# Where the next table's products stand in the block loop of a gather layer

## The chip, the cores and the metric

The kernel runs on one core of a Trainium2 chip. Its metric is the device time of one execution in microseconds, the median of several runs. PE is TensorE (PEld its weight loads), DVE is VectorE, ACT is ScalarE, POOL is GpSimd and SP is SyncE. The profiled execution has times on the chip for every instruction.

## The reference

A graph with 6,250 nodes of 256 features and 100,000 edges, sorted by destination, each edge with one of eight relation types. The part that matters here is the two-layer graph network:

```
xn = layernorm(x)
for l in 0, 1:
    W[r] = sum_b coeffs[l, r, b] * bases[l, b]        # eight 256 x 256 matrices
    h[r] = x @ W[r]                                   # 6250 x 256 each
    msg  = h[edge_type, src] / max(deg[dst], 1)
    x    = segment_sum(msg, dst) + x @ self_loops[l]  # relu behind l = 0
```

Beside it, linear attention needs, over all nodes, the sum of outer products of keys and values of xn; the rest (second layer, attention output, a routed two-matrix expert network) comes behind and is the same before and after.

## The kernel before

`h` of a layer is kept in DRAM as a table of 6272 x 8 rows of 256 floats. `startup` normalizes x, turns it and writes the first table. `gnn_first` is the first gather layer and at the same time writes the second table, that is, it multiplies each finished block of 128 nodes with the next layer's eight matrices. `gnn_second` then gathers from that table, and `experts` ends the kernel.

`gnn_first` loops over NB = 49 blocks of 128 destination nodes. The engines run their own instruction lists, in program order, and meet at semaphores. `reach(eng, sem)` waits until a semaphore has risen by one more than this engine last waited for.

- **POOL** (`Aggregate.gather`, L487) has only gathers: one indirect DMA for each 128 edges fetches their rows of the table to a ring of 16 groups of four such tiles. When the ring is full it waits, once for two groups, until PE has begun the sums of the groups that are to be overwritten.
- **SP** (`count`) passes on which groups have landed, and issues some fills with zeros.
- **DVE** makes the one-hot matrices of a block's edges (`onehots`, L510 and L514, double buffered), then `finish` (L633 to L639: degree, reciprocal, scale and add own, relu, giving `xn`) and `front` (L643, L644: bias of keys and values). `low_part` (L623) makes the low part of the split of the block's turned values, and `keys` (L628) the key features.
- **PE**, for block b: `own` (L690, self loop), `sum` (L530: four matmuls for each group, one-hot times ring, between two matmuls by zero, L523 and L537), `project` (L696: keys and values), `outer` of the block before (L703), `multiply` of the block before (L715) and `turn` (L722, two transposes of `xn`). `multiply` has four chunks of 512 columns with six matmuls each (high by high, high by low, low by high, for two halves). Two PSUM banks take the chunks in turn, so chunk 2 waits until ACT has copied chunk 0.
- **ACT**: `high_part` (L754 x1T from PSUM, L756 the rounded high part), `own_part` (L763), `keep` (L759, DMA), `store` (L769, four chunk copies, then L780, a DMA of 1024 KB to the table) and the two activations of the keys (L794, L795).

The turn of block b goes out at the end of PE's step b, and its product in step b + 1, behind the sums of block b + 1. In the last step both remaining products follow the turn. The releaser names that the trace gives for semaphores can be those of an earlier stage whose semaphore numbers are used again: `pre_bs<-in_L_gnn_bases` is a tensor of `startup`.

Of the kernel before, what the change touches and what calls it, by code (L numbers as in the profile page):

```python
# [540 lines left out]
def gnn_first(nc, g, a):  # L541
# [3 lines left out]
    with ExitStack() as ctx:  # L545
# [67 lines left out]
        @block.vector  # L613
        def _(eng):
            V = nc.vector

            def seq(ins):
                ins.then_inc(dve_own, 1)
                reach(eng, dve_own)

            def low_part(k):
                reach(eng, high_ok)
                V.tensor_tensor(low[:, k, :, :], x1T[:, k, :, :], high[:, k, :, :],  # L623
                                ALU.subtract).then_inc(low_ok, 1)

            def keys(k):
                reach(eng, er_ok)
                V.scalar_tensor_tensor(out=kf[:, k, :], in0=ke[:, k, :], scalar=1.0, in1=kr[:, k, :],  # L628
                                       op0=ALU.min, op1=ALU.add).then_inc(kf_ok, 1)

            def finish(b, k):
                reach(eng, agg.agg_ok)
                seq(V.tensor_scalar(dm[:, :], agg.pagg[:, k, D:D + 1], 1.0, None, ALU.max))  # L633
                seq(V.reciprocal(g.dinv[:, ds(b, 1)], dm[:, :]))
                reach(eng, own_ok)
                seq(V.scalar_tensor_tensor(out=xn[:, :], in0=agg.pagg[:, k, 0:D], scalar=g.dinv[:, ds(b, 1)],
                                           in1=own[:, :], op0=ALU.mult, op1=ALU.add))
                eng.sem_inc(agg.agg_free, 1)
                V.tensor_scalar(xn[:, :], xn[:, :], 0.0, None, ALU.max).then_inc(xn_ok, 1)  # L639

            def front(k):
                reach(eng, p_ok)
                V.tensor_tensor(kt[:, k, :], pk[:, 0:D], bkv[:, 0:D], ALU.add).then_inc(kt_ok, 1)  # L643
                V.tensor_tensor(vb[:, k, :, 0:P], pk[:, D:2 * D].rearrange("p (h n) -> p h n", h=H2),  # L644
                                bkv[:, D:2 * D].rearrange("p (h n) -> p h n", h=H2), ALU.add).then_inc(p_free, 1)

            def step(b, k, prev):
                agg.onehots(eng, b, seq)
                if prev:
                    low_part(1 - k)  # L650
                    keys(1 - k)
                finish(b, k)
                front(k)
                if b == NB - 1:
                    low_part(k)

            eng.sem_inc(p_free, 1)
            agg.begin(eng)
            V.memset(zrow[:, :], 0.0).then_inc(zrow_ok, 1)
            eng.wait_ge(zrow_ok, 1)  # L660
            V.memset(zrow[:, D:D + 1].bitcast(I32), SKIP).then_inc(zrow_ok, 1)
            seq(V.memset(vb[:, :, :, P:P + 2], 1.0))
            seq(V.memset(mask[:, :], 0.0))
            for h in range(P // HD):
                ins = V.memset(mask[h * HD:(h + 1) * HD, h * HD:(h + 1) * HD], 1.0)
            seq(ins)
            for h in range(H2):
                eng.wait_ge(split_ok, h + 1)
                ins = V.tensor_tensor(wlow[:, h, :], rows[:, h, :], whigh[:, h, :], ALU.subtract)
            ins.then_inc(split_ok, 1)  # L670
            eng.wait_ge(kv_in, 80)
            for b in range(NB):
                step(b, b % 2, b > 0)
            keys((NB - 1) % 2)
            agg.end(eng)

            eng.wait_ge(kv_done, 1)
            for h in range(H2):
                V.tensor_tensor(g.kvn[:, h, 0:P], pkv[:, h * D:h * D + P], mask[:, :], ALU.mult)
                ins = V.tensor_copy(ksum[:, h:h + 1], pkv[:, h * D + P:h * D + P + 1])  # L680
            seq(ins)
            for h in range(H2):
                ins = V.tensor_scalar(g.kvn[:, h, P:], mask[:, 0:P:HD], ksum[:, h:h + 1], None, ALU.mult)
            seq(ins)

        @block.tensor
        def _(eng):
            def own(b):
                for h in range(H2):
                    mm = nc.tensor.matmul(po[:, 0:D], g.xT[:, h, b * P:(b + 1) * P], ws[:, h, :], start=(h == 0), stop=(h == H2 - 1))  # L690
                mm.then_inc(own_ps, 1)

            def project(b):
                reach(eng, p_free)
                for h in range(H2):
                    mm = nc.tensor.matmul(pk[:, :], g.xT[:, h, b * P:(b + 1) * P], wkv[:, h, :], start=(h == 0), stop=(h == H2 - 1))  # L696
                mm.then_inc(p_ok, 1)

            def outer(k, last=False):
                reach(eng, kf_ok)  # L700
                n = LAST if last else P
                for h in range(H2):
                    mm = nc.tensor.matmul(pkv[:, h * D:h * D + P + 2], kf[0:n, k, h * P:(h + 1) * P], vb[0:n, k, h, :],  # L703
                                          start=False, stop=(last and h == H2 - 1), skip_group_check=True)
                if last:
                    mm.then_inc(kv_done, 1)

            def multiply(k):
                reach(eng, low_ok)
                x, w = (high[:, k, :, :], low[:, k, :, :]), (whigh, wlow)  # L710
                for n in range(2 * W):
                    reach(eng, chunk_free)
                    for h in range(H2):
                        for i, j in ((0, 0), (0, 1), (1, 0)):
                            mm = nc.tensor.matmul(pm[:, n % W, 0:CW], x[i][:, h, :], w[j][:, h, n * CW:(n + 1) * CW],  # L715
                                                  start=(h == i + j == 0), stop=(h == H2 - 1 and i == 1))
                    mm.then_inc(chunk_ok, 1)

            def turn():
                reach(eng, xn_ok)  # L720
                for h in range(H2):
                    mm = nc.tensor.transpose(pT[:, h * P:(h + 1) * P], xn[:, h * P:(h + 1) * P], g.ident[:, :])  # L722
                mm.then_inc(xT_ps, 1)

            def step(b, k, prev):
                own(b)
                agg.sum(eng, b, k)
                project(b)
                if prev:
                    outer(1 - k)  # L730
                if b < NB - 1:
                    if prev:
                        multiply(1 - k)
                    turn()
                else:
                    turn()
                    multiply(1 - k)

            reach(eng, agg.ring_ok)
            eng.wait_ge(kv_in, 80)  # L740
            eng.wait_ge(split_ok, H2 + 1)
            nc.tensor.matmul(pkv[:, 0:2], g.zero[:, :], g.zero[:, 0:2], start=True, stop=False, skip_group_check=True)
            for b in range(NB):
                step(b, b % 2, b > 0)
            multiply((NB - 1) % 2)
            outer((NB - 1) % 2, last=True)
            eng.sem_inc(agg.groups_in, -NG)

        @block.scalar
        def _(eng):  # L750
            def high_part(k):
                reach(eng, kept[k], 16)
                reach(eng, xT_ps)
                nc.scalar.copy(x1T[:, k, :, :], pT[:, 0:D].rearrange("p (h n) -> p h n", h=H2)).then_inc(x1T_ok, 1)  # L754
                reach(eng, x1T_ok)
                nc.scalar.copy(high[:, k, :, :], x1T[:, k, :, :]).then_inc(high_ok, 1)  # L756
# [22 lines left out]
                lo = W * CW if b == NB - 1 else 0  # L779
                eng.dma_start(table_rows(g, 1, b)[:, lo:], rows[:, k, lo:]).then_inc(stored[k], 16)  # L780

            def step(b, k, prev):
                if prev:
                    high_part(1 - k)
                own_part()
                if prev:
                    keep(b - 1, 1 - k)
                if b == NB - 1:
                    high_part(k)
                    keep(b, k)  # L790
                if prev:
                    store(b - 1, 1 - k)
                reach(eng, kt_ok)
                nc.scalar.activation(ke[:, k, :], kt[:, k, :], ACT.Exp)  # L794
                nc.scalar.activation(kr[:, k, :], kt[:, k, :], ACT.Relu).then_inc(er_ok, 1)  # L795

            eng.sem_inc(chunk_free, W)
            for k in range(2):
# [2 lines left out]
            eng.wait_ge(wr_in, WEIGHTS_IN)  # L801
            for h in range(H2):
                nc.scalar.copy(whigh[:, h, :], rows[:, h, :]).then_inc(split_ok, 1)
            for b in range(NB):
                step(b, b % 2, b > 0)
            store(NB - 1, (NB - 1) % 2)
            for k in range(2):
                reach(eng, stored[k], 32 if k == (NB - 1) % 2 else 16)
                reach(eng, kept[k], 16)
# [521 lines left out]
```

## Time and profile before

| what | value |
|---|---|
| three runs, median (lowest to highest) | 3634.85 us (3616.99 to 3636.49) |
| profiled execution, its own time | 3627.62 us |
| its span in the trace | 3625.9 us |
| mean granted clock of TensorE | 0.801 |
| PE busy | 2399.8 us, 66% |
| POOL busy | 1649.7 us, 45% |
| DVE, ACT busy | 915.7 us, 652.3 us |
| gathers of both layers (L487) | 1564 |

Busy time of an engine is the union of its instructions' times. A PE matmul's end is modelled, so its start is the firmer number. DMA-issuing instructions count as the queue's own (ACTq) and not as busy time, but for POOL's gathers. Times in the rows count from the span's start.

### The profile page before, as it was taken

The numbers are of one execution on the slowest core, as the hardware profiler recorded it, in microseconds if no ns is written. First come the engines' busy times: TensorE is split into PE (matmuls) and PEld (weight loads), VectorE is DVE, ScalarE is ACT, GpSimd is POOL, SyncE is SP. The second block draws the span as 40 slices with busy tenths as digits, with TensorE's granted clock in tenths as the row PEclk, the third lists the DMA queues.
The fourth block names the chain that finished last, engine by engine and source line by source line (L and its number), as shares of the span: only waits on it lengthen the run. The fifth ranks groups of instructions, "written<-read, shape, count | busy, mean of one in ns | idle before, by whom it ended". The sixth has DMA issues, their size and how long they took to land. (4 is left out here: it accounts for less than half of the span.)

```text
span 3625.9 us, 37652 instructions
## 1 busy us (share of the span) xinstructions
PE 2399.8 (66%) x9592; PEld 1739.3 (48%) x9592; DVE 915.7 (25%) x2885; ACT 652.3 (18%) x1423; POOL 1649.7 (45%) x1712
## 2 busy tenths in 40 slices
PE   6999346666666666666578356676666667657287
PEld 3777234444444444444456244454444545445065
DVE  2210112222222222222123023233332323324233
ACT  4555101110111011111111101111212112110033
POOL 0000654445444444445451646556565555652535
PEclk9999668878887888778789678777777777878577
DMA  8655533333333333333332323333333333321341
GB/s 220 231 218 195 156 95 112 106 107 103 112 102 104 103 110 109 106 103 113 100 121 75 121 77 92 89 88 91 87 90 88 89 92 89 90 84 46 128 128 53
DMA packets 155518, 401.32 MB, mean 111 GB/s; under 512 B 35102, under 2 KB 86657, under 8 KB 140348
## 3 DMA queue, kind: packets, MB, share of 16 engines
q0 software_dynamic: 81648, 219.65, 20.8%
q10 hardware_dynamic: 36156, 126.22, 9.0%
q1 hardware_dynamic: 37585, 53.92, 5.5%
q8 instruction: 58, 0.95, 0.1%
q14 instruction: 71, 0.58, 0.1%
HBM read 262.69 MB, written 141.04 MB: 111 GB/s over the span
## 5 line engine op out<-in xcount | busy, mean ns | idle before, releaser
L487 POOL DMA_INDIRECT gnn_ring<-table,g_idx x1564 | 1513.1, 967 | 1627.0 <-PE gnn_pagg L530 857.3
L530 PE MATMUL gnn_pagg<-gnn_ring,gnn_oh 128*128 x3904 | 1124.5, 432 | 427.7 <-issue 378.6
L530 PEld LDWEIGHTS gnn_pagg<-gnn_ring,gnn_oh 128*128 128x128 f32 x3904 | 775.7, 212 | 775.3 <-issue 662.9
L514 DVE TENSOR_TENSOR gnn_oh<-gnn_col,g_dst 128x256 f32<-128x256 f32 x976 | 408.3, 426 | 1803.6 <-DVEq L49 1609.9
L715 PE MATMUL gnn_pm<-gnn_whigh,gnn_high 128*128 128x512 f32 x392 | 202.4, 516 | 480.1 <-ACT gnn_rows L769 473.1
L769 ACT COPY gnn_rows<-gnn_pm 128x512 f32<-128x512 f32 x196 | 110.9, 587 | 1320.9 <-DMA pre_bs<-in_L_gnn_bases 1082.7
L715 PEld LDWEIGHTS gnn_pm<-gnn_whigh,gnn_high 128*128 128x128 f32 x392 | 94.4, 241 | 520.0 <-ACT gnn_rows L769 493.4
L1026 ACT ACTIVATE gnn_qe<-gnn_pq,gnn_bq 128x128 f32<-128x128 f32 x98 | 36.0, 368 | 1061.1 <-remote 1045.6
L715 PE MATMUL gnn_pm<-gnn_wlow,gnn_high 128*128 128x512 f32 x392 | 188.0, 480 | 0.0
L715 PE MATMUL gnn_pm<-gnn_whigh,gnn_low 128*128 128x512 f32 x392 | 186.7, 476 | 0.0
L366 PE MATMUL pre_psum<-pre_whigh,pre_high 128*128 128x512 f32 x392 | 157.5, 402 | 10.6 <-DVE pre_low L294 8.1
L366 PE MATMUL pre_psum<-pre_whigh,pre_low 128*128 128x512 f32 x392 | 153.7, 392 | 0.0
L366 PE MATMUL pre_psum<-pre_wlow,pre_high 128*128 128x512 f32 x392 | 153.3, 391 | 0.0
L417 ACT COPY pre_rows<-pre_psum 128x512 f32<-128x512 f32 x196 | 114.6, 589 | 118.1 <-PE pre_psum L366 108.4
L1131 POOL DMA_INDIRECT out<-g_xT x80 | 80.0, 1000 | 99.9 <-DVE g_xT L1208 78.8
L715 PEld LDWEIGHTS gnn_pm<-gnn_whigh,gnn_low 128*128 128x128 f32 x392 | 94.9, 242 | 25.0
L715 PEld LDWEIGHTS gnn_pm<-gnn_wlow,gnn_high 128*128 128x128 f32 x392 | 96.4, 246 | 18.7
L696 PE MATMUL gnn_pk<-gnn_wkv,g_xT 128*128 128x512 f32 x196 | 98.0, 623 | 0.0
L1125 POOL DMA_INDIRECT bucket<-rt_x,exp_posi x49 | 51.2, 1045 | 89.4 <-DVE exp_posi L1229 74.7
L366 PEld LDWEIGHTS pre_psum<-pre_whigh,pre_high 128*128 128x128 f32 x392 | 74.1, 189 | 25.1 <-DVE pre_low L294 8.5
L366 PEld LDWEIGHTS pre_psum<-pre_whigh,pre_low 128*128 128x128 f32 x392 | 73.9, 188 | 15.9
L366 PEld LDWEIGHTS pre_psum<-pre_wlow,pre_high 128*128 128x128 f32 x392 | 74.2, 189 | 14.2
(172 smaller groups left out, 2210.0 us busy)
## 6 DMA issues: line engine op xcount, KB each, us to landing
table<-pre_rows ACTq DMA_DIRECT2D x49, 1024.0 KB
table<-gnn_rows ACTq DMA_DIRECT2D x48, 1024.0 KB
gnn_ring<-table,g_idx POOLq DMA_INDIRECT x1564
pre_bs<-in_L_gnn_bases SPq DMA_DIRECT2D x64, 240.0 KB
bucket<-gnn_zrow SPq DMA_DIRECT2D x16, 650.0 KB
g_xT<-bucket SPq DMA_DIRECT2D x20, 520.0 KB, 6.3
x1T<-gnn_x1T ACTq DMA_DIRECT2D x49, 128.0 KB
gnn_x1T<-x1T ACTq DMA_DIRECT2D x49, 128.0 KB, 2.1
```

What stands on the lines that cost most here:

```text
L366: mm = nc.tensor.matmul(psum[:, n, 0:hi - lo], x[i][:, h, :], w[j][:, h, lo:hi], start=(h == i + j == 0), stop=(h == H2 - 1 and i == 1))
L417: nc.scalar.copy(rows[:, b % 2, lo:hi], psum[:, n, 0:hi - lo]).then_inc(chunk_free, 1)
L487: eng.indirect_dma_start(self.ring[:, q % RG, t, 0:D], None, self.g.table[self.l][:, :], bass.IndirectOffsetOnAxis(ap=self.g.idx[:, at:at ...
L514: self.nc.vector.tensor_tensor(self.oh[:, h, :, :], self.col[:, :].unsqueeze(1).to_broadcast([P, n, P]), self.g.dst[:, ds(q * TPG + h * n, ...
L530: mm = nc.tensor.matmul(pagg[:, k, 0:self.width], self.oh[:, h, i, :], self.ring[:, ds(q & (RG - 1), 1), t, 0:self.width].rearrange("p o n ...
L696: mm = nc.tensor.matmul(pk[:, :], g.xT[:, h, b * P:(b + 1) * P], wkv[:, h, :], start=(h == 0), stop=(h == H2 - 1))
L715: mm = nc.tensor.matmul(pm[:, n % W, 0:CW], x[i][:, h, :], w[j][:, h, n * CW:(n + 1) * CW], start=(h == i + j == 0), stop=(h == H2 - 1 and ...
L769: ins = nc.scalar.copy(rows[:, k, n * CW:(n + 1) * CW], pm[:, n % W, 0:CW])
L1026: nc.scalar.activation(qe[:, k, h, :], pq[:, h * P:(h + 1) * P], ACT.Exp, bias=bq[:, h:h + 1])
L1125: eng.indirect_dma_start(g.bucket[:, :], bass.IndirectOffsetOnAxis(ap=posi[:, b:b + 1], axis=0), r.x2[:, b, :], None).then_inc(scattered, 16)
L1131: eng.indirect_dma_start(out[:, :], bass.IndirectOffsetOnAxis(ap=xb[:, t % XS, D:D + 1].bitcast(I32), axis=0), xb[:, t % XS, 0:D], None, b ...
```

## The change

PE's step b becomes: `own(b)`, `outer` of block b - 2, `multiply` of block b - 1, `sum(b)`, `project(b)`, `turn`. So a block's product comes right behind its own turn (with only the next block's own matmuls and an older outer product between) and ahead of the next block's sums. Behind the loop follow the outer product of block NB - 2, the product and the outer product of the last block. DVE's step ends with this block's `low_part` and `keys`; before, they stood one block later, behind the one-hots. ACT's step begins with this block's `high_part`; then `own_part` of the next block, the two activations, `keep` and `store` of this block. The first `own_part` stands ahead of the loop. No buffer, no operation and no amount of data changes.

```diff
--- before.py
+++ after.py
@@ -644,15 +644,12 @@
                 V.tensor_tensor(vb[:, k, :, 0:P], pk[:, D:2 * D].rearrange("p (h n) -> p h n", h=H2),
                                 bkv[:, D:2 * D].rearrange("p (h n) -> p h n", h=H2), ALU.add).then_inc(p_free, 1)
 
-            def step(b, k, prev):
+            def step(b, k):
                 agg.onehots(eng, b, seq)
-                if prev:
-                    low_part(1 - k)
-                    keys(1 - k)
                 finish(b, k)
                 front(k)
-                if b == NB - 1:
-                    low_part(k)
+                low_part(k)
+                keys(k)
 
             eng.sem_inc(p_free, 1)
             agg.begin(eng)
@@ -670,8 +667,7 @@
             ins.then_inc(split_ok, 1)
             eng.wait_ge(kv_in, 80)
             for b in range(NB):
-                step(b, b % 2, b > 0)
-            keys((NB - 1) % 2)
+                step(b, b % 2)
             agg.end(eng)
 
             eng.wait_ge(kv_done, 1)
@@ -722,26 +718,23 @@
                     mm = nc.tensor.transpose(pT[:, h * P:(h + 1) * P], xn[:, h * P:(h + 1) * P], g.ident[:, :])
                 mm.then_inc(xT_ps, 1)
 
-            def step(b, k, prev):
+            def step(b, k):
                 own(b)
+                if b >= 2:
+                    outer(k)
+                if b >= 1:
+                    multiply(1 - k)
                 agg.sum(eng, b, k)
                 project(b)
-                if prev:
-                    outer(1 - k)
-                if b < NB - 1:
-                    if prev:
-                        multiply(1 - k)
-                    turn()
-                else:
-                    turn()
-                    multiply(1 - k)
+                turn()
 
             reach(eng, agg.ring_ok)
             eng.wait_ge(kv_in, 80)
             eng.wait_ge(split_ok, H2 + 1)
             nc.tensor.matmul(pkv[:, 0:2], g.zero[:, :], g.zero[:, 0:2], start=True, stop=False, skip_group_check=True)
             for b in range(NB):
-                step(b, b % 2, b > 0)
+                step(b, b % 2)
+            outer(NB % 2)
             multiply((NB - 1) % 2)
             outer((NB - 1) % 2, last=True)
             eng.sem_inc(agg.groups_in, -NG)
@@ -779,20 +772,15 @@
                 lo = W * CW if b == NB - 1 else 0
                 eng.dma_start(table_rows(g, 1, b)[:, lo:], rows[:, k, lo:]).then_inc(stored[k], 16)
 
-            def step(b, k, prev):
-                if prev:
-                    high_part(1 - k)
-                own_part()
-                if prev:
-                    keep(b - 1, 1 - k)
-                if b == NB - 1:
-                    high_part(k)
-                    keep(b, k)
-                if prev:
-                    store(b - 1, 1 - k)
+            def step(b, k):
+                high_part(k)
+                if b < NB - 1:
+                    own_part()
                 reach(eng, kt_ok)
                 nc.scalar.activation(ke[:, k, :], kt[:, k, :], ACT.Exp)
                 nc.scalar.activation(kr[:, k, :], kt[:, k, :], ACT.Relu).then_inc(er_ok, 1)
+                keep(b, k)
+                store(b, k)
 
             eng.sem_inc(chunk_free, W)
             for k in range(2):
@@ -801,9 +789,9 @@
             eng.wait_ge(wr_in, WEIGHTS_IN)
             for h in range(H2):
                 nc.scalar.copy(whigh[:, h, :], rows[:, h, :]).then_inc(split_ok, 1)
+            own_part()
             for b in range(NB):
-                step(b, b % 2, b > 0)
-            store(NB - 1, (NB - 1) % 2)
+                step(b, b % 2)
             for k in range(2):
                 reach(eng, stored[k], 32 if k == (NB - 1) % 2 else 16)
                 reach(eng, kept[k], 16)
```

## Rows read from the trace of the kernel before

**Rows 1.** Table of stages, chosen stretches: length, busy us of PE, PEld, DVE, ACT, POOL, granted clock, DMA share, GB/s.

```profile
480.00:1920.00 1440.00, 929.52 (x3494) 671.99 (x3495) 310.36 (x835) 169.26 (x389) 682.29 (x704) 0.81 0.33 107
...
1920.00:2010.00 90.00, 83.84 (x358) 62.67 (x356) 28.96 (x86) 20.95 (x46) 6.01 (x6) 0.99 0.23 86
...
911.00:915.00 4.00, 3.85 (x19) 2.88 (x17) 1.18 (x3) 1.66 (x5) 0.22 (x1) 1.00 0.73 295
```

**Rows 2.** Chain of waits, 480 to 1920 us: us in total, times, longest.

```profile
ACT gnn_rows L769 <- DMA pre_bs<-in_L_gnn_bases: 1082.7, 48, 45.5
...
POOL gnn_ring L487 <- PE gnn_pagg L530: 544.7, 43, 16.5
```

**Rows 3.** Timeline of POOL: start, us, what, count, idle before and its releaser.

```profile
882.38 1.13 POOL L487 DMA_INDIRECT gnn_ring<-table,g_idx  x1 [13.83 <-PE gnn_pagg L530]
...
901.54 0.95 POOL L487 DMA_INDIRECT gnn_ring<-table,g_idx  x1 [0.31 <-issue]
...
914.78 1.13 POOL L487 DMA_INDIRECT gnn_ring<-table,g_idx  x1 [12.30 <-PE gnn_pagg L530]
```

**Rows 4.** Timeline of PE, 889 to 911 us.

```profile
889.15 0.17 PE L537 MATMUL gnn_pagg<-g_zero 128*128 128x2 bf16 x1
...
891.34 0.47 PE L715 MATMUL gnn_pm<-gnn_whigh,gnn_high 128*128 128x512 f32 x1
...
893.95 0.39 PE L715 MATMUL gnn_pm<-gnn_whigh,gnn_low 128*128 128x512 f32 x1
...
905.79 0.79 PE L715 MATMUL gnn_pm<-gnn_whigh,gnn_high 128*128 128x512 f32 x1 [11.45 <-ACT gnn_rows L769]
...
906.81 0.63 PE L715 MATMUL gnn_pm<-gnn_whigh,gnn_low 128*128 128x512 f32 x1
...
907.23 0.63 PE L715 MATMUL gnn_pm<-gnn_whigh,gnn_high 128*128 128x512 f32 x1
...
910.06 0.38 PE L722 MATMUL gnn_pT<-g_ident,gnn_xn 128*128 128x128 f32 x2
...
911.14 0.17 PE L523 MATMUL gnn_pagg<-g_zero 128*128 128x2 bf16 x1
```

**Rows 5.** Timeline of ACT, 905 to 911 us.

```profile
905.15 1.07 ACT L769 COPY gnn_rows<-gnn_pm 128x512 f32<-128x512 f32 x2 [24.95 <-DMA pre_bs<-in_L_gnn_bases]
...
910.95 0.33 ACTq L780 DMA_DIRECT2D table<-gnn_rows  x1
```

**Rows 6.** Timeline of DVE, 892 to 896 us.

```profile
892.38 0.16 DVE L633 TENSOR_SCALAR gnn_dm<-gnn_pagg 128x1 f32<-128x1 f32 x1 [3.87 <-remote]
...
893.41 0.38 DVE L639 TENSOR_SCALAR gnn_xn<-gnn_xn 128x256 f32<-128x256 f32 x1
...
895.80 0.76 DVE L514 TENSOR_TENSOR gnn_oh<-gnn_col,g_dst 128x256 f32<-128x256 f32 x2 [0.40 <-issue]
```

**Rows 7.** Timeline of PE and ACT, 926 to 938 us.

```profile
926.41 0.39 PE L715 MATMUL gnn_pm<-gnn_whigh,gnn_low 128*128 128x512 f32 x1
...
932.31 0.59 ACT L769 COPY gnn_rows<-gnn_pm 128x512 f32<-128x512 f32 x1 [19.30 <-DMA pre_bs<-in_L_gnn_bases]
...
937.86 1.08 ACT L769 COPY gnn_rows<-gnn_pm 128x512 f32<-128x512 f32 x2 [4.96 <-DMA pre_bs<-in_L_gnn_bases]
```

**Rows 8.** Timeline of the loop's last block, 1992 to 2006 us.

```profile
1992.10 0.17 PE L537 MATMUL gnn_pagg<-g_zero 128*128 128x2 bf16 x1
...
1994.38 0.38 PE L722 MATMUL gnn_pT<-g_ident,gnn_xn 128*128 128x128 f32 x2
...
1994.85 0.37 ACT L754 COPY gnn_x1T<-gnn_pT 128x256 f32<-128x256 f32 x1 [9.14 <-PE gnn_pT L722]
...
1995.25 0.41 ACT L756 CAST gnn_high<-gnn_x1T 128x256 fp32r<-128x256 f32 x1
...
1995.69 0.42 DVE L623 TENSOR_TENSOR gnn_low<-gnn_x1T,gnn_high 128x256 fp32r<-128x256 f32 x1 [0.81 <-ACT gnn_high L756]
...
2005.57 0.61 PE L703 MATMUL gnn_pkv<-gnn_vb,gnn_kf 106*128 106x130 f32 x4
```

## The prediction

> **What bounds the kernel now.** I read the table of stages first [rows 1]. In the first layer's loop, 480 to 1920 us, PE is busy 929.5 of 1440 us and POOL 682.3, so no engine is full. In the 90 us behind it, where POOL issues six gathers, PE is busy for 83.8. The profiled execution took 3627.62 us with a span of 3625.9; this loop is 40% of it, and the change touches nothing else.
>
> The chain of waits says who stands still for whom [rows 2]: POOL waits 43 times for the sums, 544.7 us in all, and ACT's copies of the product chunks wait 1082.7 us for something named after a DMA of the stage before. So POOL works in bursts, one about every 1440/43 = 33.5 us. The burst of [rows 3] runs from the gather at 882.38 to the one started at 901.54: 16 gathers in 19.16 us.
>
> What ACT's copy waits for has to be found by exclusion. Its two conditions are the store of two blocks ago and the chunk itself. The store is not late: one issued at 910.95 falls into a stretch of 4 us that moves 295 GB/s, 1.18 MB, enough for its 1024 KB [rows 1, 5]. And in one block the first copy ran at 932.31 and the next at 937.86 although only the chunk's semaphore lies between them and chunk 1's last matmul was issued at 926.41 [rows 7]. So PE's completions are reported late. In the block of [rows 4, 5], chunks 0 and 1 are issued from 891.34 to 893.95, and both are copied from 905.15: 11 us later, and 3.61 us after the start of the burst's last gather [rows 3]. Where no burst runs, a turn issued at 1994.38 is copied at 1994.85 [rows 8]. Why completions are held the trace doesn't tell; that they are let go at the burst's end is what I build on. I call that moment E.
>
> One block is then: the sums start at T; the first gather at T+3.6 (911.14, 914.78 [rows 3, 4]); the last one 19.2 later; E 3.6 after that; then what PE still owes before the next sums. That last stretch is 905.15 to 911.14 here, 5.99 us, and 33.5-26.4 = 7.1 on the average. **It is exposed, and it is what the change edits.** It holds 0.64 us of copy and handoff (to 905.79), the 12 matmuls of chunks 2 and 3 (4.27 us, to 910.06), then the turn and own (1.08 us, to 911.14) [rows 4].
>
> **The change part by part: PE.** The same matmuls run per block in another order: sums, project, turn, next block's own, an outer product one block later than before, all four chunks, sums. Chunk 0 of a block now hangs on that block's own turn, x1T copy, split and low part. When is the turn done? The sums' last matmul is issued at 889.15 and reported at 892.38; the relu of xn starts at 893.41 and takes 0.38 [rows 4, 6]. So the turn goes out 11.5 us into the burst, and PE stands still before it for some 3 us; that costs nothing, as PE then has 10 us of burst to wait out. Chunk 0 of before was issued in the same place, second behind the sums, 10.3 us into the burst, and was held to E. I take it that the turn is held to E as well, and own behind it.
>
> Then, from E: copy to split 0.40 us (1994.85, 1995.25), split to low part 0.44 (to 1995.69), low part 0.42 and a handoff of about 0.07 [rows 8]: 1.33 us to the first chunk matmul. Behind it 24 matmuls instead of 12. PE has stood still for 11 us before them as it had before 905.79, and there its matmuls start 0.42 us apart (906.81, 907.23), 512 columns at the 1.2 GHz level, before they reach 0.237 (11 steps from 891.34 to 893.95) [rows 4]. That slow start is paid once in either order. So the first 12 matmuls cost 4.27 as now, the other 12 cost 12 x 0.237 = 2.84. Gone are 0.64 and 1.08. **Sum: 1.33+2.84-0.64-1.08 = +2.4 us a block.**
>
> The bounds of it: were the 12 extra matmuls all at the low level, 12 x 0.42 = 5.0 us, it would be +4.6; were all 24 at the full one, 1.33+5.7 = 7.0 against 7.1, nothing. The row at 905.79 is the nearest, as it shows a restart after the same pause.
>
> *How many blocks.* 43 bursts, but in five of them the first copy came well before the burst's usual end; the one at 932.31 is such a block [rows 7]. There the turn may be answered in time, and I take nothing for them: 38 x 2.4 = **+91 us**.
>
> *The ends of the loop.* Now two products follow the last sums, from 1992.10 to 2005.57. After the change one does: the turn at about 1993.9, the chunks 0.47+1.33 later, 24 x 0.23 = 5.5 us, so 2001.2: **-4.4 us** [rows 8]. The three blocks before, without bursts, wait 1.8 us from turn to chunks and have own and an outer product (about 1.5) to fill it: +0.3 each, +0.8. At the start the first product falls into the long first filling of the ring, in which the second block's sums waited anyway: +1.5, from 0 to 5.
>
> **DVE.** low_part and keys are moved, not added, from behind the next block's one-hots to ahead of them. Behind low_part's new wait stand keys and those one-hots, and for them the next sums. Low ends at E+1.3; keys waits for ke and kr, which ACT does behind x1T, split and own, each up to the split's 0.40, so it ends near E+2.5; from relu to the first one-hot, with two other operations between, it is 2.4 us now (893.41, 895.80) [rows 6], so the one-hot is there by E+5.4. The sums start at E+9.5. The chunks hide it; without them it would be those 5.4 us.
>
> **ACT.** Its x1T copy waits at the head of the block, with split, own, ke and kr behind, then the chunk copies: they are free at about E+2, and chunk 0 is through at E+4. The table store leaves about 1 us after the next sums have started, not 0.19 before (910.95, 911.14) [rows 4, 5]. It moves for 4 us and would overlap the burst's first 1.4 us; that bounds a late burst at +1.4, and I take 0, since the burst's pace, 19.16/15 = 1.28 us a gather, is POOL's issue and not the data's. POOL's and SP's queues keep their order.
>
> 3627.6+91-4.4+0.8+1.5 = 3716.5. The median of the runs shown lies 7 us above the profiled time, within their spread of 19.5. I predict **3718 us**.
>
> **The rivals.** *A, the turn is held to E*: above, 3718; from +1.6 to +3.6 a block, 3685 to 3765.
>
> *B, the turn comes through, own doesn't.* Completions also come singly inside a burst (932.31, two gathers before its end [rows 7]). Chunks 0 and 1 would then be done at E, but ACT owes own, ke and kr first, 1.3 us or so: E to sums 1.3+0.64+4.27 = 6.2 against 5.99 here, +0.2 a block, about 3640.
>
> *C, faster: nothing of the turn is held.* If turn and own are answered in 0.5 us as in [rows 8], chunks 0 and 1 stand ready at E, ACT owes nothing, and the sums start 0.64+4.27 later: 1.08 less a block, 43 x 1.08 = 46, less 2 at the ends: 3580. It decides once the turn and own are reported 5 us ahead of E. For it: the sums inside a burst get their answers at once, or the one-hots would not keep up. Against it: 905.15, which is what 38 of 43 blocks do. The Trainium skill (SBUF — State Buffer, Who interferes with whom) states that a DMA never contends with a compute engine, since engine and DMA ports are apart. By that rule gathers could not hold PE's work back and C would come true; the rows at 893.95 and 905.15 don't agree with so wide a reading, as something about the burst does reach PE's reports.
>
> *D, worse: the low clock lasts through the whole product.* 43 x 4.6 = 198: 3824. Against it: after 905.79 twelve matmuls took 4.27, not 5.0.
>
> **How the numbers follow.** About 0.5%, 18 us, is what a measurement can tell from no change. A 0.68, B 0.12, C 0.12, D 0.08. A rests on a row that repeats in most blocks; that the turn inherits chunk 0's fate is my inference, and B and C share what it leaves. Slower is A and D, 0.76; same is B, 0.12; faster is C, 0.12. The range leaves out C and D, 0.20, and ends a little beyond B and A: 3625 to 3775.
>
> **What would show each step.** If A is right, no chunk matmul runs inside a burst, the x1T copy comes 3.6 us after the last gather's start, and 24 chunk matmuls follow in about 7 us; POOL's waits grow from 544.7/43 = 12.7 to 15 us, the distance of bursts from 33.5 to 35.9. The stretch from the last sums to the layer's end shrinks by 4 us. I am wrong at the main step if x1T copies lie well inside the bursts (B if own's doesn't, C if both do), at the size if chunk matmuls stay 0.42 apart (D), and at the cover if the sums' first matmul waits for a one-hot.

## The result, and the profile after

The changed kernel takes **3594.66 us** (median of 8 runs, 3585.02 to 3609.15), the kernel before 3631.37 beside it (8 runs): 0.9916 of before, 95% interval 0.9891 to 0.9941. It is faster by 0.8%, where the prediction said slower. The profiled execution took 3602.8 us with a span of 3601.1, 24.8 us less span than the kernel before has in its trace.

The table of stages has the loop of the first layer (columns as in [rows 1]):

```profile
480.00:1920.00 1440.00, 993.40 (x3607) 700.30 (x3608) 324.51 (x855) 181.93 (x407) 687.51 (x710) 0.86 0.34 109
```

In the same 1440 us PE issues more matmuls than in [rows 1], 3607, at a granted clock of 0.86 instead of 0.81, and POOL more gathers, 710: more blocks go through in that time. The chain of waits of the same stretch:

```profile
POOL gnn_ring L487 <- PE gnn_pagg L530: 541.6, 47, 16.9
ACT gnn_x1T L747 <- DMA pre_rows<-wrel: 348.5, 20, 33.3
ACT gnn_rows L762 <- DMA pre_bs<-in_L_gnn_bases: 257.1, 42, 14.5
ACT gnn_x1T L747 <- PE gnn_pT L718: 231.9, 16, 16.2
ACT gnn_own L756 <- remote: 102.8, 40, 4.8
```

POOL still waits for PE's sums once a block, but ACT's wait of 1082.7 us for the chunks [rows 2] is down to 257.1. ACT now stands at the x1T copy instead, the head of its block, where the engine has nothing else to do. "remote" and the DMAs of long past stages are the profile's guesses at what released these waits; what they have in common is that a completion of PE is seen late.

The timeline of one block, POOL, PE, ACT and DVE together (start, length, engine, idle time before):

```profile
879.59 1.13 POOL L487 DMA_INDIRECT gnn_ring<-table,g_idx  x1 [11.49 <-PE gnn_pagg L530]
886.36 0.17 PE L537 MATMUL gnn_pagg<-g_zero 128*128 128x2 bf16 x1
889.59 0.16 DVE L633 TENSOR_SCALAR gnn_dm<-gnn_pagg 128x1 f32<-128x1 f32 x1 [4.54 <-remote]
891.03 0.44 PE L718 MATMUL gnn_pT<-g_ident,gnn_xn 128*128 128x128 f32 x2 [2.68 <-DVE gnn_xn L639]
893.19 0.37 ACT L747 COPY gnn_x1T<-gnn_pT 128x256 f32<-128x256 f32 x1 [16.47 <-DMA pre_rows<-wrel]
894.51 0.79 PE L711 MATMUL gnn_pm<-gnn_whigh,gnn_high 128*128 128x512 f32 x1 [1.49 <-issue]
896.69 0.37 ACT L756 COPY gnn_own<-gnn_po 128x256 f32<-128x256 f32 x1 [2.69 <-remote]
898.64 0.94 POOL L487 DMA_INDIRECT gnn_ring<-table,g_idx  x1 [0.30 <-issue]
899.31 0.39 PE L711 MATMUL gnn_pm<-gnn_whigh,gnn_low 128*128 128x512 f32 x1
902.46 1.07 ACT L762 COPY gnn_rows<-gnn_pm 128x512 f32<-128x512 f32 x2 [4.77 <-DMA pre_bs<-in_L_gnn_bases]
903.10 0.80 PE L711 MATMUL gnn_pm<-gnn_whigh,gnn_high 128*128 128x512 f32 x1 [3.40 <-ACT gnn_rows L762]
...
907.31 0.18 PE L523 MATMUL gnn_pagg<-g_zero 128*128 128x2 bf16 x1
...
908.20 0.33 ACTq L773 DMA_DIRECT2D table<-gnn_rows  x1
910.96 1.13 POOL L487 DMA_INDIRECT gnn_ring<-table,g_idx  x1 [11.38 <-PE gnn_pagg L530]
```

The burst runs from 879.59 to 898.64. The turn goes out at 891.03, and **its answer is there at 893.19, inside the burst**, 9 us before E. Own's comes at 896.69. So chunks 0 and 1 are through PE by 899.7, and they, and they alone, are held to E (902.46, 3.8 us behind the start of the last gather). From there to the sums it is 4.85 us, against 5.99 in [rows 4, 5].

Over the 44 intervals of the loop's 45 bursts, the time from a burst's first gather to the next sums adds up to 1278.8 us before and 1238.7 after: 40.1 less, 0.91 a burst. The turn's copy starts 2.2 us after the turn (median of the 42 bursts of 16 gathers), own's 5.6 us after the turn (mean).

### The profile page after: what moved, and what is told of

Its sections match the earlier page's. It is cut to its first block and busy times, and to the rows that moved or that the text cites. A ratio compares the mean times of both kernels' runs of the same rounds, so it can differ in the third digit from the quotient of the medians.

```text
span 3601.1 us, 37652 instructions
## 1 busy us (share of the span) xinstructions
PE 2442.1 (68%) x9592; PEld 1750.2 (49%) x9592; DVE 924.5 (26%) x2885; ACT 657.0 (18%) x1423; POOL 1648.2 (46%) x1712
## 5 line engine op out<-in xcount | busy, mean ns | idle before, releaser
L711 PE MATMUL gnn_pm<-gnn_whigh,gnn_low 128*128 128x512 f32 x392 | 194.7, 497 | 0.0
L762 ACT COPY gnn_rows<-gnn_pm 128x512 f32<-128x512 f32 x196 | 110.7, 587 | 449.4 <-DMA pre_bs<-in_L_gnn_bases 257.1
L747 ACT COPY gnn_x1T<-gnn_pT 128x256 f32<-128x256 f32 x49 | 18.2, 372 | 802.7 <-DMA pre_rows<-wrel 391.4
L718 PE MATMUL gnn_pT<-g_ident,gnn_xn 128*128 128x128 f32 x98 | 21.7, 304 | 98.2 <-DVE gnn_xn L639 56.3
```

The lines of the kernel that those rows point to most:

```text
L762: ins = nc.scalar.copy(rows[:, k, n * CW:(n + 1) * CW], pm[:, n % W, 0:CW])
```

## The experiments

The runs are of two kinds, and this has to be known to read them. Each set of kernels ran together on one chip, with the kernel before among them. In some sets the kernel before took 3613 to 3672 us, with bursts as above; in others some 2612 us, and POOL hardly paused. The kind was the same for every kernel and execution of a set. The chip alone doesn't settle it: chip 4 showed only bursts, 0 and 5 only the other kind, 12 each once. Every ratio below is to the kernel before in the same set. The changed kernel and the kernel before it were traced only with bursts, and the changed kernel was never timed without them.

**1. Where the gain is: only turn and own moved.** The product is the one of the block before, so two products follow the last sums again; the rest is as changed:

```
 def step(b, k):                     # PE
     own(b)
     if b >= 2:
         outer(k)
-    if b >= 1:
-        multiply(1 - k)
+        multiply(k)                 # of block b - 2
     agg.sum(eng, b, k)
...
+multiply(NB % 2)                    # behind the loop, ahead of the last product
...
-    store(b, k)                     # ACT
+    if b: store(b - 1, 1 - k)
...
+store(NB - 1, (NB - 1) % 2)         # behind the loop
```

> Changed kernel, but the product that follows a block's turn and the next own matmuls is the one of the block before (its split and low part are a block old), so only turn and own have moved out of the stretch between E (ACT's first chunk copy) and the next sums; chunks 0 and 1 are issued about 3 us earlier than in the changed kernel, and two products follow the last sums again. Theory S (the gain is the 1.08 us of turn and own that left that stretch): bursts stay 32.0 us apart as in the changed kernel, only the 4.4 us at the loop's end come back, about 3599 us. Theory P (the gain is that chunks 0 and 1 are issued later, nearer to E, so that the clock is higher at chunks 2 and 3): bursts go back toward 33.0 us, about 3630 us.

The kernel before took 2612.24 us here, turn_only 2612.61: 0.9998 [0.9989, 1.0008]. There is no burst for either theory to work on, and twice more (turn_only_b 1.0004, turn_only_c 1.0000) there was none. The timeline shows what is different there:

```profile
896.79 0.17 PE L537 MATMUL gnn_pagg<-g_zero 128*128 128x2 bf16 x1
897.02 0.16 DVE L633 TENSOR_SCALAR gnn_dm<-gnn_pagg 128x1 f32<-128x1 f32 x1 [1.54 <-PE gnn_pagg L537]
898.62 0.38 PE L718 MATMUL gnn_pT<-g_ident,gnn_xn 128*128 128x128 f32 x2
899.09 0.37 ACT L747 COPY gnn_x1T<-gnn_pT 128x256 f32<-128x256 f32 x1 [12.16 <-PE gnn_pT L718]
```

Gathers come every 1.25 us all the time, and yet each answer of PE is there at once, 0.23 us after the sums' end and 0.47 after the turn. Reports are not held there, whatever POOL does. PE is then busy 677.0 of the 720 us from 480 to 1200, at a granted clock of 0.99.

> The kernel of turn_only again, for executions in which the kernel before takes some 3625 us and works in bursts; its first runs fell among executions of 2612 us, where it could tell nothing of bursts. Theory S (the gain is the 1.08 us of turn and own that left the stretch from E to the next sums): bursts 32.0 us apart as in the changed kernel, only the 4.4 us at the loop's end come back, 0.993 of before. Theory P (the gain is that chunks 0 and 1 are issued some 5 us later, nearer to E): 33.0 us apart, 1.000 of before.

> The kernel of turn_only a third time, since both times before it ran where the kernel before takes 2612 us and gathers never pause. If it meets executions of some 3625 us with bursts: theory S (turn and own left the stretch from E to the sums), bursts 32.0 us apart, 0.993 of before; theory P (chunks 0 and 1 nearer to E), 33.0 us apart, 1.000 of before. If not, 1.000 again.

> The changed kernel once more, in the company in which the first four experiments ran: there the kernel before took 2612 us, not 3631. If gathers come without a pause (no burst, no held reports), the 1.08 us of turn and own have no exposed stretch to leave, and only the shorter end of the loop is left of the change: 4.4 us less, 0.998 of before. If it runs in bursts as in the first result, 0.992. Were the gain there made by the order of the products in itself, it would show here too, some 25 us less.

> The kernel before once more, for its trace. If reports of TensorE's completions are held only in some executions, then in one of 2612 us the first chunk copy follows its chunk by less than 1 us and POOL never waits more than some 2 us for the sums; in one of 3630 us the copy comes 22.8 us after the burst's first gather, as before.

These two met bursts: 3593.98 us and 0.9927 [0.9901, 0.9953]; before_again took 3626.66 us in its one execution, and in 34 of its 42 bursts of 16 gathers the first chunk copy comes 22.7 to 22.9 us after the first gather, as expected for 3630 us. The result repeats.

> The changed kernel a third time, beside turn_only. Where gathers never pause and the kernel before takes 2612 us: theory S says that only the loop's shorter end is left, 0.998 of before (5 us less); a gain of the order in itself would be 0.991. Where it works in bursts: 0.992 again.

> The kernel of turn_only a fourth time. In executions with bursts theory S says 32.0 us from burst to burst and 0.993 of before, theory P 33.0 us and 1.000. In executions without, 1.000 again.

Both in one set, with bursts: after_c 3596.77 us, 0.9907 [0.9890, 0.9924]; turn_only_d 3600.07 us, 0.9918 [0.9901, 0.9934]. That is theory S, not P: its bursts are 32.11 us apart on the average (before 32.81, the three traces of the changed kernel 31.84 to 32.14). The end of the loop is 13.6 us again from the last sums' end to the last copy, against 9.4. But the start of the loop is shorter, 78.5 us from the first sums to the first burst behind the filling against 83.8 in after_c, so that the two loops last nearly as long, 1571.2 and 1574.5 us. Theory S had counted the end alone; that 3599 was met so closely is in part luck. The first chunk of turn_only_d is issued 12.2 us into the burst instead of 14.2 (medians), which makes no difference:

```profile
819.97 0.44 PE L718 MATMUL gnn_pT<-g_ident,gnn_xn 128*128 128x128 f32 x2 [1.14 <-issue]
821.54 0.38 ACT L747 COPY gnn_x1T<-gnn_pT 128x256 f32<-128x256 f32 x1 [14.33 <-PE gnn_pT L718]
823.62 0.37 ACT L756 COPY gnn_own<-gnn_po 128x256 f32<-128x256 f32 x1 [1.27 <-remote]
824.09 0.39 PE L711 MATMUL gnn_pm<-gnn_whigh,gnn_low 128*128 128x512 f32 x1
829.20 0.95 POOL L487 DMA_INDIRECT gnn_ring<-table,g_idx  x1 [0.30 <-issue]
832.86 1.07 ACT L762 COPY gnn_rows<-gnn_pm 128x512 f32<-128x512 f32 x2 [8.25 <-DMA pre_bs<-in_L_gnn_bases]
833.50 0.79 PE L711 MATMUL gnn_pm<-gnn_whigh,gnn_high 128*128 128x512 f32 x1 [9.03 <-ACT gnn_rows L762]
```

Turn and own are answered at 821.54 and 823.62; the chunks, last issued at 824.09, are copied at 832.86, again 3.66 us after the start of the last gather.

**2. The stretch by itself.** Own once more, for nothing, behind chunk 3:

```
     if b >= 1:
         multiply(1 - k)
+        own(b, again=True)      # no semaphore
```

> Changed kernel with the four own matmuls issued once more, for nothing, behind chunk 3 and ahead of the next sums. Theory S (what stands in the stretch from E to the sums is paid in full in each of the blocks with a burst): 0.65 us more a block, 43 times 0.65 = +28 us, about 3623 us. Theory P (the stretch has slack, the clock made the gain): no more than 5 us, about 3597 us.

> The kernel of own_again again, for executions in bursts. Theory S: 0.65 us more a block than the changed kernel, 28 us, 1.000 of before. Theory P: 0.992 to 0.994.

No bursts either time: 1.0075 twice, 20 and 19 us over the kernel before for four matmuls in each of 48 blocks. If the changed kernel without them takes what the kernel before takes, which no run measured, that is 0.4 us a block. It suggests that PE's time is exposed there, and says nothing of the stretch behind E.

**3. No pause before E.** 24 matmuls of zeros between chunks 1 and 2:

```
 for n in range(2 * W):
+    if n == W:
+        for _ in range(24):
+            nc.tensor.matmul(pkv[:, 0:P], g.zero[:, :], g.zero[:, 0:P], start=False, stop=False, ...)
     reach(eng, chunk_free)
```

> Changed kernel with 24 small matmuls of zeros (128 columns, bf16, added to the key-value sums) between chunks 1 and 2, so that TensorE does not stand still while it waits for E. Theory W (chunks 2 and 3 start slowly because TensorE stood still before them): their 12 matmuls go 0.24 us apart from the start, 2.9 instead of 4.2 us, in the blocks in which the filler ends before E: up to 1.3 us less a block, 43 times 1.3 = 56 less, 3540 to 3560 us. Rival (the slow start has nothing to do with the pause, or the filler runs past E): 3590 to 3640 us. If reports of completion were served one matmul after another, the filler would delay the report of chunks 0 and 1, and ACT's first copy would come later than 22.8 us after the burst's start.

> The kernel of fill24 again, for executions in bursts (with gathers without a pause the filler cost 48 us, one a block). Theory W (the pause before E makes chunks 2 and 3 start slowly): up to 1.3 us less a block than the changed kernel, 0.975 to 0.985 of before. Rival (the filler runs past E, or the start is slow anyway): 0.990 to 1.005. If TensorE's completions are served one after another, the first chunk copy comes later than 22.8 us after the burst's start.

> The kernel of fill24 a third time, for executions in bursts. Theory W (the pause before E makes chunks 2 and 3 start slowly): up to 1.3 us less a block than the changed kernel, 0.975 to 0.985 of before. Rival, from banks3_d's trace, where answers are held and TensorE is not slow: 24 matmuls more before E are harmless, but theory Q says that each adds to what is held, so E or the first chunk copy comes later than 22.8 us after the burst's start: 0.995 or more. Without bursts 1.018 again.

Three times it met executions without bursts: 1.0183, 1.0187 and 1.0189, 47 to 48 us over the kernel before. What a filler does in a burst stays untried.

**4. A third chunk inside the burst.** Three banks of PSUM for the chunks; po and pT share one, so own stands behind the wait for the low part:

```
-pm = s.ps("pm", [P, W, 512])
+pm = s.ps("pm", [P, 3, 512])       # chunk n of block b in bank (2 * W * b + n) % 3
-pT = s.ps("pT", [P, 512])
+pT = po[:, D:2 * D]
...
     reach(eng, low_ok)             # PE, multiply(b)
+    if b < NB - 1: own(b + 1)
...
     keep(b, k)                     # ACT
+    if b < NB - 1: own_part()
     store(b, k)
...
-eng.sem_inc(chunk_free, W)
+eng.sem_inc(chunk_free, 3)
```

> Changed kernel with three banks of PSUM for the chunks instead of two, so chunk 2 too can be issued inside the burst; own stands behind the wait for the low part, and ACT copies it behind ke and kr, just ahead of chunk 0. Theory R (TensorE works at its normal pace inside a burst and only the reports of its completions are held until E): chunks 0 to 2 are ready at E, 6 matmuls instead of 12 are left, 1.4 to 2.6 us less, 0.4 more for ACT's copy of own at E; the sums start 1 to 2 us earlier, 43 times 1 to 2, 3510 to 3550 us. Theory L (TensorE itself is slow inside a burst): chunk 2 is not through at E and nothing is gained, 3590 to 3620 us.

> The kernel of banks3 again, for executions in bursts. Theory R (only reports are held, until E): chunk 2 is ready at E too and 6 matmuls are left: sums 1 to 2 us earlier in each block, 0.970 to 0.982 of before. Theory L (TensorE itself is slow inside a burst): chunk 2 isn't through at E, 0.99 to 1.00.

> The kernel of banks3 a third time. If it meets executions with bursts: theory R (TensorE works at its pace and only its reports are held until E), chunk 2 is ready at E and 6 matmuls are left, 0.970 to 0.982 of before; theory L (TensorE itself is slow inside a burst), chunk 2 isn't through at E, 0.99 to 1.00. If not, 1.007 again.

Without bursts: 1.0069, 1.0070 and 1.0060, 17 us slower than the kernel before. PE now waits 1.0 us a block for the low part ahead of own (34.0 us in 35 blocks of the chain of waits).

> The kernel of banks3 once more, hoping for executions in bursts (before near 3625 us). Theory R (TensorE works at its pace inside a burst and only reports of completion are held until E): chunk 2 is ready at E too and 6 matmuls instead of 12 are left behind it, 1 to 2 us less a block, 0.970 to 0.982 of before. Theory L (TensorE itself is slowed inside a burst, so that more matmuls there only come later): chunk 2 isn't through at E, 0.99 to 1.00. Without bursts 1.006 again.

With bursts: **3531.98 us against 3661.65, 0.9638 [0.9605, 0.9671]**, more than theory R asked for. The timeline of a block:

```profile
802.06 0.44 PE L721 MATMUL gnn_po<-g_ident,gnn_xn 128*128 128x128 f32 x2 [2.72 <-DVE gnn_xn L639]
805.00 0.37 ACT L751 COPY gnn_x1T<-gnn_po 128x256 f32<-128x256 f32 x1 [17.62 <-DMA pre_rows<-wrel]
806.32 2.08 PE L686 MATMUL gnn_po<-gnn_ws,g_xT 128*128 128x256 f32 x4 [3.07 <-issue]
807.83 0.99 PE L714 MATMUL gnn_pm<-gnn_whigh,gnn_high 128*128 128x512 f32 x1
...
809.41 0.39 PE L714 MATMUL gnn_pm<-gnn_whigh,gnn_high 128*128 128x512 f32 x1
809.64 0.39 PE L714 MATMUL gnn_pm<-gnn_wlow,gnn_high 128*128 128x512 f32 x1
809.90 0.95 POOL L487 DMA_INDIRECT gnn_ring<-table,g_idx  x1 [0.30 <-issue]
...
812.61 0.39 PE L714 MATMUL gnn_pm<-gnn_whigh,gnn_low 128*128 128x512 f32 x1
813.47 0.37 ACT L760 COPY gnn_own<-gnn_po 128x256 f32<-128x256 f32 x1 [7.04 <-remote]
813.74 1.57 ACT L766 COPY gnn_rows<-gnn_pm 128x512 f32<-128x512 f32 x3
814.38 0.50 PE L714 MATMUL gnn_pm<-gnn_whigh,gnn_high 128*128 128x512 f32 x1 [1.38 <-ACT gnn_rows L766]
814.72 0.39 PE L714 MATMUL gnn_pm<-gnn_wlow,gnn_high 128*128 128x512 f32 x1
...
815.88 0.18 PE L523 MATMUL gnn_pagg<-g_zero 128*128 128x2 bf16 x1
```

Of the 18 matmuls of three chunks all but the first three start 0.23 us apart, from 809.41 on, while gathers are still under way, and from E on own and all three chunks are copied without a pause, 813.47 to 815.31. PE itself was not slow; only its answers were held. Six matmuls are left, and they start 0.34 and 0.23 us apart, not 0.59 and 0.43 as in the changed kernel (903.10, 903.69, 904.12). The tables of stages show the clock of it, the changed kernel's chunks 2 and 3 first, then banks3_d's chunk 3:

```profile
903.10:906.10 3.00, 3.00 (x7) 2.43 (x8) 0.00 (x0) 0.47 (x2) 0.00 (x0) 0.51 0.00 0
906.10:907.40 1.30, 1.30 (x8) 0.86 (x7) 0.00 (x0) 0.55 (x1) 0.00 (x0) 1.00 0.00 0
```

```profile
814.30:815.90 1.60, 1.52 (x7) 1.07 (x7) 0.00 (x0) 1.01 (x3) 0.00 (x0) 1.00 0.00 0
```

A granted clock of 0.51 is the 1.2 GHz level, 1.00 that of 2.4. PE had stood still for 3.4 us before the first and for 1.4 us before the last. Over the bursts with all four copies, first copy to sums is 2.61 us on the average in banks3_d, 5.37 in the changed kernel: 2.8 us less, where the expectation had 1 to 2. In the two blocks shown, the changed kernel's first six matmuls behind E take 2.72 us (903.10 to 905.82) and banks3_d's only six 1.50 (814.38 to 815.88); so about half of the gain there is the six matmuls that are gone and half the clock of those that are left.

**5. Shorter chunks in the burst.** turn_only with chunks 0 and 1 cut to the high by high product:

```
-for i, j in ((0, 0), (0, 1), (1, 0)):
+for i, j in ((0, 0), (0, 1), (1, 0)) if n >= W else ((0, 0),):
```

> The kernel of turn_only with chunks 0 and 1 cut from 6 matmuls each to 2 (the two correction terms with a low part are left out of these two chunks; chunks 2 and 3 are whole), so that chunk 0 is done well before the middle of the burst. Theory R, strong form (a chunk's report waits for the burst's end whatever its length): the first copy still comes 22.8 us after the burst's start, bursts 32.1 us apart as in turn_only, 0.992 of before. Theory L (what is held up is work, matmul by matmul, some 0.7 us each): 8 matmuls fewer, so the first copy comes 17 to 20 us after the burst's start, chunk 2 starts inside the burst and the next sums come up to 4 us earlier, 0.95 to 0.97 of before. Without bursts the 8 matmuls are 1.8 us less for TensorE in each block.

In the set of banks3_d, with bursts: 3614.98 us, 0.9866 [0.9835, 0.9897]; bursts 32.09 us apart on the average, as in turn_only_d (32.11):

```profile
825.69 1.18 PE L711 MATMUL gnn_pm<-gnn_whigh,gnn_high 128*128 128x512 f32 x4
...
830.62 0.37 ACT L756 COPY gnn_own<-gnn_po 128x256 f32<-128x256 f32 x1 [3.39 <-remote]
831.85 1.04 POOL L487 DMA_INDIRECT gnn_ring<-table,g_idx  x1 [0.31 <-issue]
835.64 1.07 ACT L762 COPY gnn_rows<-gnn_pm 128x512 f32<-128x512 f32 x2 [4.03 <-DMA pre_bs<-in_L_gnn_bases]
```

Four matmuls instead of twelve, done at 826.9, and they are answered at E all the same, 8.8 us later. So the chunks' own matmuls are not what their answers wait for. It does not rule out theory L, though: the own matmuls stand ahead of chunk 0, and their answer came 6.2 us after their issue (824.46), 18.7 us into the burst in the median of 42 (16.4 in turn_only_d, in another set). If answers come in order, chunk 0's, six matmuls behind own's, had 4 us left until E, which is what L's 0.7 us a matmul asks for; the expectation of 17 to 20 us had not counted that own would be late.

**6. Does every matmul cost an answer?** turn_only with 8 tiny matmuls without a semaphore ahead of own:

```
+if b >= 1:
+    for _ in range(8):
+        nc.tensor.matmul(pkv[:, 0:2], g.zero[:, :], g.zero[:, 0:2], start=False, stop=False, ...)
 own(b)
```

> The kernel of turn_only with 8 matmuls of zeros on 2 columns (no semaphore, nothing waits for them) between the turn and the own matmuls, 8 times some 0.06 us of TensorE's time. In turn_only ACT copied own 3 to 6 us after own's issue in bursts. Theory Q (inside a burst the answer to each matmul costs some 0.7 us, with a semaphore or without): own's copy comes 5 us or more later, near E, in most blocks; the time stays within 0.5% of turn_only's. Theory M (only the messages of semaphores are slow there): own's copy comes when it did, 3 to 6 us after own's issue. Without bursts some 0.5 us of TensorE more a block.

It met executions without bursts: 1.0013 [1.0003, 1.0023], which says nothing on Q or M. The first filling of the ring says more on them (below).

## Why the prediction was wrong, step by step

**The step that failed** is "I take it that the turn is held to E as well, and own behind it." The turn stands where chunk 0 stood, 11.5 us into the burst, and is answered 2.2 us later, own some 3 us behind it. "Chunk 0 was issued in the same place and was held" is true, and still didn't carry over: a completion isn't held to E for being issued so far into a burst. The sums' end itself could have warned: it was issued 6.8 us into the burst and answered 3 us later [rows 4, 6], so not everything in a burst was held to its end. In the block above, the answers to sums' end, turn and own come some 3, 2 and 4 us late, and chunk 0's 5 us, as it is through PE only at about 897.2; where it was issued earlier it just waits longer (in turn_only_d 10 us, from 822.9 to 832.86).

What fits the traces with bursts is a line: answers come in order, slowly, and what still stands in it near the burst's end comes at E. Chunk 0 of the kernel before stood 14 matmuls behind the sums' end in that line; the turn now stands six behind it. The kernel before shows it in its 42 bursts of 16 gathers. In six, the one of [rows 7] among them, the sums' end was answered after 0.24 us, and just these six have chunk 0 copied ahead of E, 13.6 to 21.0 us into the burst. In the other 36 the sums' end was answered 1.5 to 4.6 us late and chunk 0 was copied at 22.7 to 22.8. No experiment varied this alone, so it stays a reading of traces.

Rival C, with 0.12, had the outcome: turn and own answered well ahead of E, though not after 0.5 us as it had assumed. turn_only_d shows that this alone makes the gain.

**What held.** The frame did: the period is sums to burst, burst, E, and the stretch behind E. E itself stayed 22.8 us behind the first gather. Out of the stretch went the turn and own, 1.08 us by C's working, and 0.91 measured. The slow start at 903.10 costs what it did, 4.21 us for the 12 matmuls against 4.27. It is met twice now, as the matmuls of chunks 0 and 1 also start 0.43 us apart (895.10 to 898.94), but inside the burst, where it is hidden. The end of the loop was forecast at -4.4 and is -4.3. DVE's and ACT's moves were hidden, as the step on them said. One reading was off without harm: 1440/43 divides by the waits in the table, while the bursts themselves start 32.81 us apart, so the stretch behind E averages 6.4 us, not 7.1; the sum went by the rows of one block.

**Sizes in C.** C said 3580. The parts, from the two traces: -40.1 for the stretches (C: -46); +5.4 from the sums' start to the first gather, which in about half the blocks is now 3.7 to 4.1 us instead of 3.64. The table store now leaves 0.9 us behind the sums' start (908.20), so it may be that, as the step on ACT had bounded it at +1.4 and taken as 0; no run takes it apart. The last blocks without full bursts gave +2.7 (forecast +0.8), the loop's end -4.3, and **the start +7.4 (85.9 us instead of 78.5 from the first sums to the first burst behind the filling), where I had +1.5 with a bound of 5**. Together -28.9, which is the loop's measured difference, 1600.1 to 1571.2 us from the first sums to the last copy. (The span is only 24.8 us shorter, as the changed kernel's first sums came 3.5 us later and what follows the loop took 0.6 us more.) The start was mis-sized because the first filling of the ring is a burst four times as long, and there the answers are later still, so that the first product, which now hangs on its own turn, comes late; turn_only_d, where it doesn't, has 78.5 us again:

```profile
421.57 0.17 PE L537 MATMUL gnn_pagg<-g_zero 128*128 128x2 bf16 x1
435.73 0.16 DVE L633 TENSOR_SCALAR gnn_dm<-gnn_pagg 128x1 f32<-128x1 f32 x1 [15.42 <-remote]
437.11 0.69 PE L718 MATMUL gnn_pT<-g_ident,gnn_xn 128*128 128x128 f32 x2 [13.55 <-issue]
446.23 0.42 DVE L643 TENSOR_TENSOR gnn_kt<-gnn_pk,gnn_bkv 128x256 f32<-128x256 f32 x1 [9.18 <-DMA wrel<-pre_xs]
452.59 0.37 ACT L747 COPY gnn_x1T<-gnn_pT 128x256 f32<-128x256 f32 x1 [42.83 <-DMA pre_rows<-wrel]
463.73 0.37 ACT L756 COPY gnn_own<-gnn_po 128x256 f32<-128x256 f32 x1 [10.33 <-remote]
480.59 0.59 ACT L762 COPY gnn_rows<-gnn_pm 128x512 f32<-128x512 f32 x1 [14.46 <-DMA pre_bs<-in_L_gnn_bases]
```

The sums' end is answered 14 us late, the turn 15.5, own 25. The steps between the answers go by the number of matmuls: 10.5 us to the keys' and values' (L643, four matmuls), 6.4 to the turn's (two), 11.1 to own's (four), 16.9 to chunk 0's (six), 2.6 to 3.2 us each, with one semaphore message in every step. That is what theory Q says, at another price than 0.7 us, and not theory M. And the wait goes on without gathers: the last one starts at 477.19, and chunk 1, issued by 458.76, is copied at 486.84.

The other traces with bursts show the same steps where they can be read, 2.3 to 3.2 us a matmul.

The turn is this late in two places, here and in the burst of 24 gathers, where the turn at 1762.04 is copied at 1774.01. Here it isn't held to the end, as the gathers go on for another 25 us; there it comes 1.3 us after the last gather's start. So rival A, the turn held to E, came close to being real once, and nowhere else. The trace of the kernel before had shown as much for the turn itself, in its own first filling, which goes on until 474.02:

```profile
434.32 0.69 PE L722 MATMUL gnn_pT<-g_ident,gnn_xn 128*128 128x128 f32 x2 [10.76 <-issue]
450.50 0.37 ACT L754 COPY gnn_x1T<-gnn_pT 128x256 f32<-128x256 f32 x1 [5.18 <-DMA pre_rows<-wrel]
```

**The rule against the trace.** The Trainium skill (SBUF — State Buffer, Who interferes with whom) states that a DMA never contends with a compute engine. For the matmuls banks3_d agrees, 0.23 us apart while gathers run. It doesn't cover the completions: 8.8 us late in short, inside a burst, and 0.47 us without.

**What stays open.** Why the completions are late, why only in some sets, and why all that are left come together at E in a burst of 16. That each matmul costs the time, and not each semaphore message, is read from the first filling; experiment 6, made to test it, met no burst. In the bursts of 16 the price is less even: in the changed kernel it is 1.4 to 5.6 us from the turn's answer to own's, four matmuls.

## What to carry to other kernels

When completions come late while another engine is bursting, read how late each one is, in their order, before carrying the fate of one over to another that is moved to its place. Look for the operation to be moved in the trace of before, wherever it already stands in such a stretch. Where only the last ones are held, put as much finished work as the buffers hold in front of the release: here the new order took 0.8% off, and the new order with a third bank 3.6%, each in its own set. And see whether other executions run in the same way before tuning for a wait: where no answer was held, the kernel with the third bank was 0.6 to 0.7% slower than the one before.

## What the runs showed of the hardware

- The kernel before took 2612 us in some sets and 3613 to 3672 in others, a factor of 1.4, with nothing changed. In turn_only's trace, of the first kind, PE's completions are seen by ACT and DVE 0.23 to 0.5 us after the issue. In the traces of the second kind most are seen 1 to 13 us after it in bursts of 16 gathers, which are issued 1.25 us apart, and up to 25 us (own) in the first filling. In a burst of 16, those still out come together, 3.6 to 3.8 us after the start of the last gather; its last data are in 2.4 us after that start (901.1 in the block shown, behind which the table of stages has no DMA until 902.4), so they come some 1.2 us behind the landing.
- Completions of ACT and DVE were not late in the same bursts: in the changed kernel the low part waits for the split and the first chunk for the low part, and from the x1T copy (893.19) to that chunk (894.51) it is 1.32 us; the prediction had added up 1.33 from [rows 8], which lie outside a burst.
